# GpSimd takes over the sum of the weights' magnitudes, normalising goes ahead of the weight splits, and the attention stage gets a new table

## The reference

```python
xn = _layernorm(x)
# attention, 32 heads of 32
qkv = clip(xn @ Wqkv.T, -8, 8); q, k, v = split(qkv, 3)
q = layer_norm(q, q_ln_w, q_ln_b); k = layer_norm(k, k_ln_w, k_ln_b)
scores = q . k * 32**-0.5 + slopes[h] * (pos_k - pos_q)     # causal
out = softmax(scores) @ v @ Wout.T
# FFN with a binarised weight
alpha = mean(abs(W), axis=1); W_b = alpha * sign(W)
ffn = xn @ W_b.T + bias
return x + out + ffn
```

## Time and profile before

| | us |
|---|---|
| median of 3 runs | 1409.92 (1408.61 to 1413.5) |
| the profiled execution | 1414.06 |
| its span, first to last instruction | 1412.3 |
| TensorE busy | 1341.1 (95%) |
| VectorE busy | 791.2 (56%) |
| ScalarE busy | 512.0 (36%) |
| GpSimd busy | 446.0 (32%) |
| mean granted TensorE clock | 0.993 |

### The profile page before, as it was taken

How to read it: one execution, slowest core, us unless ns; L and a number is a source line. 1 busy time by engine, 2 the same in 40 slices (tenths; PEclk the granted TensorE clock), 3 DMA queues, 4 the chain that set the end, 5 groups by cost and what they waited for, 6 DMA issues and landing times.

```text
span 1412.3 us, 36370 instructions
## 1 busy us (share of the span) xinstructions
PE 1341.1 (95%) x15012; PEld 678.3 (48%) x15012; DVE 791.2 (56%) x1794; ACT 512.0 (36%) x1019; POOL 446.0 (32%) x313
## 2 busy tenths in 40 slices
PE   5799999999999999699999999989999999999998
PEld 2344444444454444244345555555555555444443
DVE  4677266655566661112578778878877788201111
ACT  5444111111111110000037767767777777700000
POOL 1222000000000000000005555555544445697665
PEclk9999999999999999899999999999999999999999
DMA  5445122223222225712122333332333332144543
GB/s 214 156 158 198 70 53 67 67 72 77 61 74 67 70 71 134 195 68 81 54 62 57 90 87 81 89 79 79 84 89 87 87 87 60 46 170 136 165 148 119
DMA packets 143799, 137.99 MB, mean 98 GB/s; under 512 B 81969, under 2 KB 110769, under 8 KB 143474
## 3 DMA queue, kind: packets, MB, share of 16 engines
q1 hardware_dynamic: 79199, 99.55, 23.3%
q10 hardware_dynamic: 64467, 36.50, 10.1%
HBM read 93.42 MB, written 42.21 MB: 96 GB/s over the span
## 4 chain that ended last, share of the span: by engine, by line
PE 77%; DMA 9%; DVE 6%; issue 3%; ACT 2%; SPq 2%; POOL 0%; DVEq 0%; ACTq 0%; POOLq 0%
PE ps L1029 49%; PE ps L1099 7%; PE ps L1160 6%; DMA arena<-arena 5%; PE ps L1183 5%; PE ps L1188 4%; DVE ps L931 2%; PE ps L1076 2%; PE ps L1163 1%; DMA arena<-q_scr 1%; SPq L357 1%; PE ps L1193 1%; DMA v_scr<-arena 1%; ACT arena L663 1%; PE ps L1018 1%
## 5 line engine op out<-in xcount | busy, mean ns | idle before, releaser
L1029 PE MATMUL ps<-arena 128*128 128x512 f16 x3584 | 792.7, 381 | 17.9 <-DVE arena L890 11.8
L1029 PEld LDWEIGHTS ps<-arena 128*128 128x128 f16 (+1 forms) x3584 | 348.8, 98 | 437.2 <-issue 17.3
L740 ACT ACTIVATE arena<-ps 128x512 f32<-128x512 f32 (+3 forms) x768 | 339.6, 498 | 146.0 <-PE ps L1163 92.9
L599 POOL TENSOR_TENSOR arena<-arena 128x2048 f32<-128x2048 f32 (+1 forms) x48 | 201.8, 4204 | 390.8 <-ACT arena L740 388.4
L931 DVE CUSTOM_DVE_ANT_0 ps<-ps,arena 128x128 f32<-128x128 f32 (+3 forms) x512 | 239.4, 518 | 58.2 <-PE ps L1099 56.0
L1160 PE MATMUL ps<-arena 128*32 128x512 f16 (+3 forms) x3072 | 255.3, 327 | 4.0 <-ACT arena L740 2.5
L1099 PE MATMUL ps<-arena 127*32 127x512 f16 (+3 forms) x3072 | 237.3, 327 | 14.7 <-DVE arena L931 10.2
L648 ACT ACTIVATE arena<-arena 128x512 f32 (+1 forms) x64 | 40.1, 629 | 492.2 <-DMA arena<-in_wqkv_t 317.0
L890 DVE TENSOR_SCALAR arena<-ps 128x1024 f32<-128x1024 f32 x48 | 58.8, 1225 | 216.9 <-PE ps L1029 187.6
L935 DVE TENSOR_REDUCE arena<-ps 128x1 f16<-128x512 f32 x256 | 162.9, 682 | 15.7 <-PE ps L1099 15.7
L1183 PE MATMUL ps<-arena 128*32 128x512 f32 (+3 forms) x1536 | 160.8, 485 | 0.5 <-issue 0.3
(11 more groups left out here) (53 smaller groups left out, 785.9 us busy)
## 6 DMA issues: line engine op xcount, KB each, us to landing
arena<-in_x SPq DMA_DIRECT2D x32, 512.0 KB, 5.3
arena<-in_wqkv_t SPq DMA_DIRECT2D x48, 256.0 KB, 2.9
arena<-k_scr ACTq DMA_DIRECT2D x39, 256.0 KB
base_scr<-arena SPq DMA_DIRECT2D x16, 512.0 KB, 2.9
v_scr<-arena SPq DMA_DIRECT2D x16, 512.0 KB, 2.9
arena<-r_scr SPq DMA_DIRECT2D x32, 256.0 KB
arena<-base_scr SPq DMA_DIRECT2D x16, 512.0 KB, 4.4
out_dram<-arena SPq DMA_DIRECT2D x16, 512.0 KB, 6.2
```

Of the source, the lines that this page charges most:

```text
L599: nc.gpsimd.tensor_tensor(acc[:, :, at:HALF], former, p32[k % PSLOTS][:, :, 0:w], ALU.add)\
L740: nc.scalar.activation(p32[k % PSLOTS][:, j, 0:w], ps[:, TRB[x % RB], 0:w], ACT.Exp, scale=SCALE).then_inc(exp_done, 1)
L1029: ins = nc.tensor.matmul(dst[c], lhs(k, a), wparts[:, k, b, c * HALF:(c + 1) * HALF], start=(k == 0 and (a, b) == order[0]), stop=(k == KT ...
```

## The change

- The sum of magnitudes goes from VectorE to GpSimd. A magnitude is now weight times sign (`magnitude`, written over `wf`), and `sum_up` adds it. The first two are done ahead of the loop; in the loop, which is now written out, `magnitude(i+1)` stands behind `f_step(2i)` and `sum_up(i+1)` behind `f_step(2i+1)`.
- ScalarE: `normalize_x(t+1)`, then `xt_high(t)`, then `split_hi(t)`; `xt_high(0)` one sign earlier.
- VectorE: `split_lo` of the tile before instead of the same tile's; `abs_sum` is gone.
- SP: x2 is loaded ahead of the last two weight tiles; in the loop x first, then w of two tiles before, then the store.
- Attention: new `NATS` and `PV_AFTER`; `recips` behind items 18 and 34 instead of 22 and 32; `row_a_in` ahead of `recips_in(n-1, 1)`; `o_norm`, `o_low` and `o_high` one chunk later, `os_copy(n-1, 1)` ahead of `o_high(n-1, 0)`; stack parts behind chunks 1 to 8 instead of 3 to 10, v behind chunk 9 instead of 2.

```diff
-        NATS = [3, 4, 3, 4, 2, 5, 3, 4, 5, 3, 3, 3]
+        NATS = [3, 4, 3, 4, 2, 5, 3, 5, 4, 4, 3, 2]
-        PV_AFTER = {(0, 2): [-2], (2, 1): [-1], (3, 0): [0], (4, 2): [1], (5, 2): [2], (6, 2): [3],
-                    (7, 1): [4], (8, 2): [5], (9, 1): [6], (10, 0): [7], (11, 0): [8], (11, 2): [9]}
+        PV_AFTER = {(0, 2): [-2], (2, 1): [-1], (3, 0): [0], (4, 2): [1], (5, 2): [2], (6, 1): [3],
+                    (7, 1): [4], (7, 3): [5], (8, 3): [6], (10, 0): [7], (10, 3): [8], (11, 2): [9]}
...
# SP
                 sp.dma_start(wf[:, j, :], wffn_t[j * P:(j + 1) * P, :]).then_inc(wf_ld[j], 16)
-            load_x(2, 0, 1)
+                if j == KT - 3:
+                    load_x(2, 0, 1)
...
-            load_w(Q, 2, 0, 1)
             with sp.Fori(1, NT // 2 - 1) as j:
-                load_w(Q, j * 2 + 1, 1, j)
-                load_x(j * 2 + 2, 0, j + 1)
-                store_base(j * 2 - 2, 0)
-                load_w(Q, j * 2 + 2, 0, j + 1)
-                load_x(j * 2 + 3, 1, j + 1)
-                store_base(j * 2 - 1, 1)
-            load_w(Q, NT - 1, 1, NT // 2 - 1)
+                for p in range(2):
+                    load_x(j * 2 + 2 + p, p, j + 1)
+                    load_w(Q, j * 2 + p, p, j)
+                    store_base(j * 2 - 2 + p, p)
+            for t in range(NT - 2, NT):
+                load_w(Q, t, t % 2, t // 2)
...
                 if n > 0:
                     sums_out(blk_no(n - 1, 1))
-                    recips_in(blk_no(n - 1, 1))
                 if n < GROUPS - 1:
                     row_a_in(n + 1)
+                if n > 0:
+                    recips_in(blk_no(n - 1, 1))
                 sums_out(blk_no(n, 0))
...
# GpSimd
+            def magnitude(j):
+                nc.gpsimd.tensor_tensor(wf[:, j, :], wf[:, j, :], wsl[F][:, j, 0, :], ALU.mult).then_inc(abs_done, 1)
+            def sum_up(j):
+                pool.wait_ge(abs_done, j + 1)
+                pool.wait_ge(asum_done, j)
+                nc.gpsimd.tensor_tensor(asum, asum, wf[:, j, :], ALU.add).then_inc(asum_done, 1)
             for t in range(2):
                 f_step(t, t)
-            with pool.Fori(1, NT // 2) as i:
-                for p in range(2):
-                    f_step(i * 2 + p, p)
+            pool.wait_ge(sign_done, 1)
+            nc.gpsimd.tensor_tensor(asum, wf[:, 0, :], wsl[F][:, 0, 0, :], ALU.mult).then_inc(asum_done, 1)
+            pool.sem_inc(abs_done, 1)
+            pool.wait_ge(sign_done, 2)
+            magnitude(1)
+            sum_up(1)
+            pool.wait_ge(sign_done, KT)
+            for i in range(1, NT // 2 - 1):
+                f_step(i * 2, 0)
+                magnitude(i + 1)
+                f_step(i * 2 + 1, 1)
+                sum_up(i + 1)
+            for t in range(NT - 2, NT):
+                f_step(t, t % 2)
...
-                        if c == 1:
+                        if c == 2:
                             o_norm(n - 1, 0)
-                        if c == 4:
+                        if c == 5:
                             o_low(n - 1, 0)
-                        if c == 7:
+                        if c == 8:
                             o_norm(n - 1, 1)
...
# ScalarE
-                if j == 2:
+                if j == 1:
                     xt_high(0, 0)
...
             normalize_x(2, 0, 1)
             for t in range(2):
                 split_hi(Q, t, t, 0)
+            normalize_x(3, 1, 1)
+            xt_high(2, 0)
             split_hi(Q, 2, 0, 1)
             with act.Fori(1, NT // 2 - 1) as j:
-                for t, p, m in ((j * 2 + 1, 1, j), (j * 2 + 2, 0, j + 1)):
-                    xt_high(t - 1, 1 - p)
-                    split_hi(Q, t, p, m)
-                    normalize_x(t, p, m)
-            xt_high(NT - 2, 0)
+                for p in (1, 0):
+                    normalize_x(j * 2 + 3 - p, 1 - p, j + 1)
+                    xt_high(j * 2 + 2 - p, p)
+                    split_hi(Q, j * 2 + 2 - p, p, j + 1 - p)
+            xt_high(NT - 1, 1)
             split_hi(Q, NT - 1, 1, NT // 2 - 1)
-            normalize_x(NT - 1, 1, NT // 2 - 1)
-            xt_high(NT - 1, 1)
...
-                            if (c, j) == (2, 0):
+                            if (c, j) == (3, 0):
                                 o_high(n - 1, 0)
                             if (c, j) == (2, 1):
                                 os_copy(n - 1, 1)
-                            if (c, j) == (10, 3):
+                            if (c, j) == (11, 3):
                                 o_high(n - 1, 1)
-                            if (c, j) == (2, 3) and n < GROUPS - 1:
+                            if j == 3 and 0 < c <= LOADS and n + 2 < GROUPS:
+                                load_part(act, n + 2, c - 1)
+                            if (c, j) == (LOADS + 1, 3) and n < GROUPS - 1:
...
                                 load_vg(act, n + 1)
-                            if j == 3 and 3 <= c < 3 + LOADS and n + 2 < GROUPS:
-                                load_part(act, n + 2, c - 3)
...
# VectorE
             def f_step(t, p, m, last=False):
+                def former():
+                    split_lo(Q, t - 1, 1 - p, m if p else m - 1)
                 if last:
-                    split_lo(Q, t, p, m)
+                    former()
                 else:
...
-                    statistics(t + 1, 1 - p, lambda: split_lo(Q, t, p, m))
+                    statistics(t + 1, 1 - p, former)
                 x_low(t, p)
                 f_out(t - 2, p, m - 1)
                 xt_low(t, p)
-                if p and not last:
-                    abs_sum(m + 1)
...
-            dve.wait_ge(sign_done, 1)
-            nc.vector.scalar_tensor_tensor(asum, wf[:, 0, :], -1.0, wf[:, 0, :], ALU.mult, ALU.max).then_inc(asum_done, 1)
-            dve.sem_inc(abs_done, 1)
             xt_low(1, 1)
-            dve.wait_ge(sign_done, KT)
-            abs_sum(1)
...
-            split_lo(Q, 2, 0, 1)
...
+            split_lo(Q, NT - 1, 1, NT // 2 - 1)
...
-                    if pos == 22 and n > 0:
+                    if pos == 18 and n > 0:
                         recips(n - 1, 1)
-                    if pos == 32:
+                    if pos == 34:
                         recips(n, 0)
```

More of the change, by code:

```diff
@@ L832, in x_low @@
                 nc.vector.tensor_tensor(xl[p], u[p], xh[p], ALU.subtract).then_inc(xl_done, 1)
-            def abs_sum(j):
-                tile = wf[:, bass.ds(j, 1), :].rearrange("p o n -> p (o n)")
-                nc.vector.scalar_tensor_tensor(tile, tile, -1.0, tile, ALU.mult, ALU.max).then_inc(abs_done, 1)
-                dve.wait_ge(abs_done, j + 1)
-                dve.wait_ge(asum_done, j)
-                nc.vector.tensor_tensor(asum, asum, tile, ALU.add).then_inc(asum_done, 1)
             def f_step(t, p, m, last=False):
+                def former():
+                    split_lo(Q, t - 1, 1 - p, m if p else m - 1)
                 if last:
-                    split_lo(Q, t, p, m)
+                    former()
                 else:
```

2 lines of the change are left out of this document (added).

## The result

The changed kernel takes **1374.57 us** (median of 4 runs, 1373.84 to 1377.71), the kernel before 1411.71 (1408.61 to 1417.46) beside it. The ratio is 0.9737 (95% interval 0.97 to 0.9774), 37 us less. The profiled execution took 1374.1 us with a span of 1372.3, which is 40.0 us less than the span before. The terms of the sum are measured against these 40.0 us.

A forecast was written before the change was run, and what follows sets the result against it. TensorE, busy 95% of the span, was taken as the bound, so only its idle time could be won. Terms 15.0 + 12 + 1 = 28 us took 1409.9 to 1382 us; bounds 1377.4 to 1394.6, 80% range 1376 to 1393.

The forecast's parts named there:

- First stage: Tiles up to `turn_x(15)`: removing TensorE's waits for VectorE's `x_low` gains 15.0 us together, bounds 11.3 to 16.5.
- The steady part: First stage, `turn_x(5)` to `turn_x(15)`: TensorE runs at its own 7.80 us a tile, 78.0 instead of 84.6, gain 6.6 us.
- product 2: Early first stage: starts between 33.3 and 34.8 us, taken as 34.8 because GpSimd's small instructions wait for VectorE's.
- port: First stage rival: GpSimd's long instruction delays L832 or L803 in each tile; 1388 to 1390 us, chance 0.12.
- Attention: Attention stage: earlier sums and stack loads remove TensorE's long waits, 12 us of 13.2, bounds 4 and 15.
- the floor: Attention stage: a group without a gap lasts 31.63 us, as 970.25 to 1001.88.
- Stack loads: Attention stage: issued 5 us before the end of the group's loads, they end TensorE's three `q_scr` waits, 3.0 us.
- Table: Attention stage: five items instead of four in chunk 7 cost 0 to 0.5 us per group, taken as 0.1.
- VectorE's backlog: Attention rival: the gap only moves, 0.6 us stay in each of 14 groups; 20 us gained, 1390, chance 0.13.
- Last group: End of attention: `o_high(14, 1)` behind the last exponentials removes TensorE's 1.04 us gap at 1239.31, gain 1 us.
- The slower rival: Attention: second-half sums too late for item 18; gain gone at 10.8 us transfer, 1427 us at 12; chance 0.03.
- That the early order gains nothing: Early first stage rival: another operand of product 2 or 3 is last, half clock follows; 8 us less, 1390, chance 0.06.

The follow-up runs named there:

- sum_alone: Kernel before with only the sum of magnitudes moved to GpSimd, every other order as before: 1400.4 us, ratio 0.993 to the kernel before.
- order_alone: Kernel after with the sum back on VectorE, all new orders, loads and attention stage kept: 1385.7 us, ratio 0.9802 to the kernel before.
- old_loads: Kernel after with stack loads behind chunks 3 to 10 and the v load behind chunk 2 again: 1383.3 us, ratio 0.9809 to the kernel before.
- f_loads: Kernel after with the old attention stage except the new places of stack loads and v load: 1399.6 us, ratio 0.9899 to the kernel before.
- old_recips: Kernel after with reciprocals behind items 22 and 32 and SP's old order, new table and loads kept: 1414.5 us, ratio 1.0027 to the kernel before.

## Why the prediction was wrong in size, point by point

The forecast was 28 us less. The larger part of the error is the attention stage, 9.6 us; the first stage adds 1.7.

**First stage, 15.0 predicted, 16.7 measured: mechanism right, one term too small.** The steady part was forecast at 7.80 us a tile and 6.6 us, and it is. `turn_x(2)` came at 31.23 (31.1). The step that failed is product 2: "I take 34.8, since L551 was the one that waited at 103.64". It started at 33.40, next to my lower bound of 33.3, so the term was taken 1.4 us too late. The timeline of the kernel after, all engines:

```profile
28.15 0.20 POOL L551 TENSOR_TENSOR small<-small 128x1 f32<-128x1 f32 x1
28.17 1.31 DVE L823 SCALAR_TENSOR_TENSOR arena<-arena 128x512 f16<-128x512 f32 x2 [6.19 <-ACT arena L668]
...
29.02 0.52 POOL L554 TENSOR_TENSOR small<-small 128x1 f32<-128x1 f32 x1
29.41 1.21 DVE L852 TENSOR_TENSOR arena<-arena 128x1024 f16<-128x1024 f32 x1
29.49 3.35 POOL L563 TENSOR_TENSOR arena<-arena 128x1024 f32<-128x1024 f32 x1
29.62 1.24 ACT L683 ACTIVATE arena<-arena,small 128x1024 f32<-128x1024 f32 x1 [0.96 <-issue]
```

GpSimd's small instructions got in at 28.15, 0.02 us ahead of VectorE's first two-input instruction, and were through at 29.54; I had them wait for all three. The two behind L551 were held a little (0.64 and 0.52 us, against 0.19 each in the tile before). The long sum, L563, took 3.35 us instead of 2.37 beside VectorE's L852, and nobody needs it. So `turn_x(3)` came at 38.59 (39.9) and `turn_x(4)` at 44.07 (45.6). The gap ahead of it, 2.69 us (2.9), had the clock at full, as I took it (1.00 from 40 to 52 us). 1.5 of the missing 1.7 us are here.

**The rival that the chances call port, GpSimd's long instruction in front of L832 or L803 in each tile, did not come true.** The steady tile of the kernel after:

```profile
102.90 1.17 DVE L852 TENSOR_TENSOR arena<-arena 128x1024 f16<-128x1024 f32 x1
103.06 1.06 POOL L542 TENSOR_TENSOR small<-small 128x1 f32<-128x1 f32 x1 [3.28 <-DVE small L835]
...
105.38 2.37 POOL L563 TENSOR_TENSOR arena<-arena 128x1024 f32<-128x1024 f32 x1
...
106.77 1.23 DVE L841 COPY arena<-ps 128x1024 f32<-128x1024 f32 x1 [2.69 <-PE ps L1038]
```

L852 takes 1.17 us; the one that waits is GpSimd's one-column L542, 1.06 us, and it ends with L852. The long sum lies beside L841, which reads PSUM and keeps its 1.23 us. This is the place in the tile that the prediction gave it. That one of the two waits for the other is in these rows; that a port is behind it is in none. Moving the sum to GpSimd helped: `sum_alone` gained 12.6 us in this stage, and in the new order, too, the sum off VectorE is worth 10.1 us at `turn_x(15)` (139.92 less 129.87) and 11 to 12 us in all (`order_alone` 1385.7 less 1374.6; spans 1384.3 less 1372.3).

**Attention, 12 predicted, 21.6 measured: the step that failed is the size of what there was to win.** The sequence of events was right, nearly to the instruction. Where the kernel before had the lines of the earlier trace rows, the kernel after has, in the group that starts at 799.43 (SP's queue, ScalarE's copy of the sums, VectorE's reciprocals):

```profile
813.45 0.24 DVE L987 RECIPROCAL arena<-arena 128x16 f32<-128x16 f32 x1
...
813.72 0.32 SPq L459 DMA_DIRECT2D r_scr<-arena  x1
...
816.22 0.63 ACT L769 ACTIVATE arena<-ps 128x512 f32<-128x512 f32 x1
816.87 0.54 SPq L454 DMA_DIRECT2D arena<-arena  x1
...
824.65 0.25 DVE L987 RECIPROCAL arena<-arena 128x16 f32<-128x16 f32 x1
```

SP issues the reciprocal's store 14.3 us into the group (forecast 14.4), `sums_out(n, 0)` right behind L769 at 17.44 us, 2.68 earlier than before (forecast 2.7), and VectorE reads at 25.2 us (forecast 25.2) without a wait. But I took as the prize "12 us of the 13.2", the waits of TensorE over 250 ns, and as the floor a group of 31.63 us. Neither was the whole: the groups hold 21.6 us, 14.5 of idle time and 7.1 of busy time, as shown above. The busy time is where the short waits are. The weight loads' list has some that are too short for the matmuls' list. Kernel before, groups 1 to 14 (us in total, times, longest), behind VectorE's copies and the stack loads:

```profile
PEld ps L1099 <- DVE arena L931: 18.4, 31, 2.0
...
PEld ps L1099 <- DVE arena L935: 5.5, 27, 0.2
...
PEld ps L1099 <- DMA arena<-q_scr: 4.0, 3, 2.2
PEld ps L1107 <- DVE arena L935: 2.7, 13, 0.2
```

and the kernel after, the same groups:

```profile
PEld ps L1108 <- DVE arena L940: 4.2, 15, 0.3
PEld ps L1116 <- DVE arena L944: 2.9, 14, 0.2
PEld ps L1108 <- DVE arena L944: 2.6, 14, 0.2
```

30.6 us against 9.7. This places the loss but doesn't size it, since a weight load's wait can lie beside a running matmul (in the kernel before one waited 0.20 us for L935 up to 969.11, with TensorE busy for all 2.00 us from 968 to 970): the list's lines behind ScalarE grew from 21.4 to 36.5 us and those of "issue" fell from 84.2 to 60.2. VectorE's own wait for the sums, at L978, follows the size group by group: 29.3 us in 13 waits in groups 1 to 14 of before and none in those of after. It was there also in groups that I read as without a gap. Kernel before, in the group of 31.77 us, and in group 14:

```profile
1009.51 0.25 DVE L978 RECIPROCAL arena<-arena 128x16 f32<-128x16 f32 x1 [1.54 <-DMA arena<-arena]
...
1203.06 0.25 DVE L978 RECIPROCAL arena<-arena 128x16 f32<-128x16 f32 x1
```

The groups of before line up with it: 31.08 us in group 14, the only one where VectorE didn't wait (it issues no stack loads either, but in the kernel after that group is only 0.02 us shorter than the others); 31.5 to 31.8 in the three (1, 8 and 13) where it waited 1.4 to 1.6 us and the list of TensorE's waits shows nothing; 32.2 to 32.7 in three (5, 11 and 12) where it waited 2.1 to 2.6; 32.9 to 33.4 in four (2, 3, 6 and 9) where it waited 2.8 to 3.3. The other three (4, 7 and 10) have waits for the stack loads as well. So the wait left a tail: the items behind it came one by one just as TensorE asked for them. The floor that I had taken was a group with 1.4 us of this wait in it.

**Stack loads, priced at 3.0 us**, are worth 8 to 9 in the kernel after (`old_loads`), and nothing beside the old table and reciprocals (`f_loads`). The new reciprocals alone, beside the old table and loads, were not tried, nor the new places of `o_norm`, `o_low` and `o_high`. I costed each edit against the kernel before and added the prices; in this stage they don't add. **Table, priced at 0.1 us a group:** right in the kernel after (0.01), while it costs 1.2 us a group (32.37 to 33.60) without the rest. The rival of **VectorE's backlog**, that the gap only moves, comes true in none of the groups of after; beside the old reciprocals the table makes the gap longer. **Last group, 1 us:** the wait of the earlier trace rows is gone, and behind group 14 the kernel is 1.3 us shorter. It was not tried by itself.

**The slower rival** needed the sums of (n-1, 1) to take 10.8 us. They land 3.1 to 3.6 us after their issue, in spite of the loads of chunks 1 to 3, and are read 7.2 us after it. It was far from deciding, and the loads of chunks 1 to 3 cost this transfer nothing that shows: before it took 3.0 to 4.4 us. I had written that it ran alone there; the v load was issued 0.6 us ahead of it (at 792.50). **That the early order gains nothing** is refuted: order beside sum gives 4.1 us at `turn_x(15)`.

**The range** took the list's 13.2 us plus a little as its end (15). An end worked out from the groups' lengths would have held the result: the shortest of before, 31.08 us, against the mean of 32.53 makes 20 us, which is known as the right floor only now.

## What to carry to other kernels

Before pricing a stall of the bounding engine, compare the lengths of equal loop passes, split into idle and busy time, and look for a pass in which the helper engine behind the stall didn't wait: here the list of long waits showed 13 us in 14 groups, and the passes held 21.6. Take parts of a schedule apart in both surroundings, since a table that is worth 0 beside the new reciprocals cost 14 us beside the old ones, and the same loads 0 or 9. And read what stands ahead of a short store in an issuing queue: 24 load issues in front of one cost 11 us of waiting and 1.7 us of half clock.

## What the runs showed of the hardware that I had not expected

- **Which engine waits where both have two inputs in SBUF** was in these rows the one that started second, even by a few hundredths: GpSimd's L551 took 0.20 us when it started 0.02 us ahead of VectorE's L823, and 1.06 us before when it started behind L832. At 103.06 GpSimd's L542, started 0.16 us behind VectorE's L852, took 1.06 us.
- **A gap of TensorE and the clock behind it.** `turn_x` took 1.05 us behind the gap of 2.69 us in the kernel after, 1.74 behind 3.69 (sum_alone), 1.86 behind 5.07 (order_alone) and 1.87 behind 6.38; before had a 2.49 us gap with half clock behind it. The length alone doesn't say which gap: `turn_x(2)` of order_alone took 1.89 us behind a gap of 2.42 (clock 0.51 from 34.5 to 36 us), and in old_recips half clock (0.50) followed one of 2.05 (830.88), while before had a gap of 2.62 us (34.17) with full clock behind it (1.00 from 30 to 43 us). The tile behind such a gap took 9.46 us (sum_alone), 9.74 (order_alone) and 10.34 (before) instead of 7.80, so shortening it brought 1.7 to 2.5 us more than the gap itself.
- **GpSimd's 128x1024 instructions** took 2.37 us for f32 plus f32 and 2.14 us for f32 times an f16 sign, and 3.35 us once, when it started 0.08 us behind VectorE's L852 of 1.21 us.
- **The same 8 KB transfer** of the sums landed after 3.1 to 3.6 us for one half and after 4.2 to 6.9 us for the other, at different places of the same group; the loads in flight beside them differ, but that they are the cause was not tried. In group 14, which issues no stack loads, they landed after 1.8 and 3.4 us.
